# A graph kernel on one core: in both edge loops, TensorE's signals move from the last matmul to a drain behind it

## What is computed

```python
# layer 0, per edge: 8 heads of 16 features
Q, K, V = x @ WQ, x @ WK, x @ WV ;  Eh = edge_attr @ WE
score = exp(clip(sum_head(K[src] * Q[dst] / 4 * Eh), -5, 5))
h = x + segment_sum(V[src] * score, dst) / (segment_sum(score, dst) + 1e-6)
x1 = layernorm(x + batchnorm(h))
# layer 1: graph attention with a softmax over each destination's edges
xl = x1 @ W ;  e = leaky_relu((xl @ att_src)[src] + (xl @ att_dst)[dst])
m = segment_max(e, dst) ;  p = exp(e - m[dst])
out = segment_sum(p / (segment_sum(p, dst)[dst] + 1e-16) * xl[src], dst) + bias
# two dense layers with batch norm and relu follow, and a last layernorm
```

## Time and profile before

| | us |
|---|---|
| median of 3 runs | 5886.87 (5868.76 to 5905.33) |
| profiled execution | 5881.81 |
| its span | 5879.8 |
| busy: TensorE, VectorE, GpSimd, ScalarE | 3739.5, 3231.2, 3271.3, 1157.5 |

### The profile page before, as it was taken

One profiled execution on the slowest core, in us unless ns is written; L12 is line 12 of the kernel. 1 busy time (PEld: TensorE's weight loads), 2 busy tenths in 40 slices (PEclk: granted clock), 3 DMA queues, 4 the chain that ended last, 5 costly groups with the idle time before them and its releaser, 6 DMA issues. The chain is left out here.

```text
span 5879.8 us, 84494 instructions
## 1 busy us (share of the span) xinstructions
PE 3739.5 (64%) x20678; PEld 2886.8 (49%) x20679; DVE 3231.2 (55%) x9533; ACT 1157.5 (20%) x4808; POOL 3271.3 (56%) x3437
## 2 busy tenths in 40 slices
PE   7666656666676666666684656666666566666577
PEld 5444444444454444545453445444444444444455
DVE  4555555555565555555562555555555555555566
ACT  3111111111111111111111222222222222222234
POOL 4555555555555555555535466666666666666641
PEclk8777777777767677766777555555555555555558
DMA  6444444444454444444423222222222222222213
GB/s 234 136 133 138 134 135 136 134 137 140 138 142 134 135 139 132 137 135 139 137 91 115 71 51 50 51 50 50 50 50 50 50 51 50 50 50 51 50 37 136
DMA packets 433128, 592.20 MB, mean 101 GB/s; under 512 B 210923, under 2 KB 291125, under 8 KB 430949
## 3 DMA queue, kind: packets, MB, share of 16 engines
q0 software_dynamic: 132560, 328.87, 21.8%
q1 hardware_dynamic: 298678, 255.32, 15.8%
q10 hardware_dynamic: 1840, 7.43, 0.3%
HBM read 556.41 MB, written 34.03 MB: 100 GB/s over the span
## 5 line engine op out<-in xcount | busy, mean ns | idle before, releaser
L415 POOL DMA_INDIRECT kv_g<-kv_table,idx x1641 | 1559.3, 950 | 1336.6 <-PE ps_sum L507 774.9
L1168 POOL DMA_INDIRECT xg<-xl_table,idx x1661 | 1582.5, 953 | 990.0 <-issue 466.0
L1226 PE MATMUL ps_sum<-pw,xg 128*128 128x64 f32 x3328 | 819.2, 428 | 475.8 <-DVE pws L1367 338.1
L1226 PEld LDWEIGHTS ps_sum<-pw,xg 128*128 128x128 f32 x3328 | 741.0, 328 | 637.7 <-DVE pws L1367 427.0
L507 PE MATMUL ps_sum<-kv_g,hot 128*64 128x136 f32 x3328 | 388.1, 371 | 955.6 <-ACT qw L584 868.4
L507 PEld LDWEIGHTS ps_sum<-kv_g,hot 128*64 128x64 f32 x3328 | 245.1, 176 | 1068.2 <-ACT qw L584 946.1
L489 PE MATMUL ps_pair<-w,eat 128*128 128x128 f32 x3328 | 693.5, 373 | 0.0
L674 DVE TENSOR_TENSOR acc<-acc,ps_turn 128x128 f32 x416 | 119.5, 287 | 1016.7 <-remote 641.8
L489 PEld LDWEIGHTS ps_pair<-w,eat 128*128 128x128 f32 x3328 | 590.1, 267 | 114.2 <-issue 114.2
L1217 PE MATMUL ps_tops<-ident,col 64*128 64x64 f32 x832 | 285.5, 445 | 304.4 <-DVE col L1345 185.2
L1262 ACT COPY third<-newm 128x64 f32 x416 | 102.4, 246 | 1816.5 <-remote 991.2
(11 more groups left out here) (174 smaller groups left out, 5344.9 us busy)
## 6 DMA issues: line engine op xcount, KB each, us to landing
eat<-in_edges SPq DMA_DIRECT2D x416, 256.0 KB
local<-local_table SPq DMA_DIRECT2D x832, 64.0 KB
xg<-xl_table,idx POOLq DMA_INDIRECT x1661
kv_g<-kv_table,idx POOLq DMA_INDIRECT x1641
xw<-in_xt SPq DMA_DIRECT2D x416, 32.0 KB
adw<-ad_row SPq DMA_DIRECT2D x416, 32.0 KB
kv_table<-kv_out SPq DMA_DIRECT2D x25, 512.0 KB
xl_table<-xl SPq DMA_DIRECT2D x25, 264.0 KB, 2.6
```

The lines of the kernel that those rows point to most:

```text
L415: nc.gpsimd.indirect_dma_start(out=kv[:, u, k, 0:2 * D], out_offset=None, in_=m["kv_table"], in_offset=bass.IndirectOffsetOnAxis(ap=idx[:, ...
L1168: nc.gpsimd.indirect_dma_start(out=xg[:, u, k], out_offset=None, in_=m["xl_table"], in_offset=bass.IndirectOffsetOnAxis(ap=idx[:, u // B, ...
L1226: nc.tensor.matmul(ps_sum[:, b, 0:W], xg[:, u, k, 0:D], pw[:, b, k], start=(k == 0), stop=(k == K - 1))
```

## The change

In five places a drain is put on TensorE behind the last matmul of a group, and the signal moves from the matmul to the drain: `q_made`, `summed` and `turned` in `edges0`, `turned` and `summed` in `edges1`. A drain is an instruction of the engine's sequencer that ends when the engine has finished what was issued to it. No matmul, wait, buffer or transfer is changed. The signals outside the two loops' bodies (the stage ahead of the second loop, the two first `spread_out`, the last `spread_max`) stay on matmuls.

```diff
@@ make_q (edges0)
                 for half in range(2):
-                    mm = nc.tensor.matmul(ps_own[at(half, W)], xw[:, u % 4], m["w"][:, WQ], start=True, stop=True)
-                mm.then_inc(q_made, 1)
+                    nc.tensor.matmul(ps_own[at(half, W)], xw[:, u % 4], m["w"][:, WQ], start=True, stop=True)
+                nc.tensor.drain().then_inc(q_made, 1)
@@ sum_up (edges0)
-                        mm = nc.tensor.matmul(ps_sum[at(half, W), b, 0:D + H], hot[:, u % 4, half * 2 + j], kv[:, u, half * 2 + j, D:ROW0],
-                                              start=(j == 0), stop=(j == K // 2 - 1))
-                mm.then_inc(summed, 1)
+                        nc.tensor.matmul(ps_sum[at(half, W), b, 0:D + H], hot[:, u % 4, half * 2 + j], kv[:, u, half * 2 + j, D:ROW0],
+                                         start=(j == 0), stop=(j == K // 2 - 1))
+                nc.tensor.drain().then_inc(summed, 1)
@@ turn_sums (edges0)
-                nc.tensor.matmul(ps_turn[0:H, b, W:2 * W], sums[:, b, D:D + H], halves[:],
-                                 start=True, stop=True).then_inc(turned, 1)
+                nc.tensor.matmul(ps_turn[0:H, b, W:2 * W], sums[:, b, D:D + H], halves[:], start=True, stop=True)
+                nc.tensor.drain().then_inc(turned, 1)
@@ turn_top (edges1)
-                nc.tensor.matmul(ps_top[0:W, u % 2, 0:P], top[:, u % 2], m["ident"][:], start=True, stop=True).then_inc(turned, 1)
+                nc.tensor.matmul(ps_top[0:W, u % 2, 0:P], top[:, u % 2], m["ident"][:], start=True, stop=True)
+                nc.tensor.drain().then_inc(turned, 1)
@@ sum_up (edges1)
-                nc.tensor.matmul(ps_sum[:, b, W:2 * W], ones, pws[:, b], start=True, stop=True).then_inc(summed, 1)
+                nc.tensor.matmul(ps_sum[:, b, W:2 * W], ones, pws[:, b], start=True, stop=True)
+                nc.tensor.drain().then_inc(summed, 1)
```

## The result

| | kernel before | changed kernel |
|---|---|---|
| median (5 runs each), us | 5881.0 (5868.8 to 5905.3) | 5918.9 (5918.2 to 5930.0) |
| ratio | 1 | 1.0065 (95% interval 1.0039 to 1.0091) |
| profiled execution: span, us | 5879.8 | 5916.8 |

Where an execution took over 1.5% more than the fastest of its kernel, the tables leave it out; further down that is one of e1's four (4775.7 us, the one profiled) and one of e6's two (4357.5 us, the one profiled).

What follows compares the result with a forecast made beforehand. A lockstep of gathers and held TensorE signals was taken to bound both loops; 615 + 383 + 40 = 1038 us off 5881.8 gives 4844, so 4850 us for the median, range 4590 to 6100.

Steps and rivals of the forecast that it cites:

- what bounds the kernel: Both loops: lockstep; gathers hold back the signal summed, then GpSimd idles for it, 2.0 and 1.06 us a chunk.
- GpSimd's two rows, 0.95 and 0.30 us: Both loops: a gather's duration and the idle time ahead of it, so four gathers need 5.0 us a chunk.
- I take it that it escapes: Both loops: a drain-given signal uses the sequencer's way and is not held under gathers; 4850 us, chance 0.60.
- 615 + 383 + 40 us: Savings forecast for the first loop, the second loop and the buffered chunks behind the last gather; 1038 us in all.
- B: Rival, both loops: the drain itself is held and TensorE stands still; 1.5 us a chunk, 620 us; chance 0.12.
- later groups run on: Argument against the held-drain rival: the matmul's data must be there, since TensorE's later groups continue.
- A: Rival, both loops: the drain's signal is held like the matmul's; drains add 243 us, 6130 us; chance 0.20.
- C: Rival: signals come at once, but TensorE's first loop falls to 1.2 GHz, 6.9 us a chunk; 5420 to 5500 us; chance 0.08.
- A drain's cost: TensorE, both loops: 0.15 to 0.45 us each, taken as 0.3; 0.9 us a chunk in the first, 0.6 in the second.
- about 6 us: First loop: TensorE's chunk at 1.2 GHz, from 4.94 us for 27 of 36 matmul records.
- The first loop without late signals: First edge loop with drains and prompt signals: 5.5 us a chunk instead of 7.0, saving 615 us.
- The second: Second edge loop with drains and prompt signals: 5.1 us a chunk instead of 6.06, saving 383 us.

Runs made afterwards that it cites:

- e1: Only the first loop's three signal-giving drains added to the kernel before, second loop unchanged; prompt signals: 4658.0 us against 4542.0, ratio 1.025.
- e6: The changed kernel with its five drains, gathers replaced by plain loads of fixed rows (outputs not the reference's); late job: 4264.4 us against 5812.9, ratio 0.734.
- e5: The kernel before, signals on matmuls, gathers replaced by plain loads of fixed rows (outputs not the reference's); late job: 3892.7 us against 5812.9, ratio 0.670.
- e12: Kernel before plus a signal-less drain behind each of the five groups, signals staying on matmuls; late job: 5930.7 us against 5885.1, ratio 1.008.
- e13: Kernel before with one first-loop drain a chunk, signalling for turn_sums and make_q together, summed on its matmul; late job: 5864.6 us against 5885.1, ratio 0.996.
- e8: Kernel before plus the first loop's three drains and two of four line 489 matmuls issued twice; late job: 5943.7 us against 5812.9, ratio 1.024.
- e2: Only the second loop's two signal-giving drains added to the kernel before, first loop unchanged; prompt signals: 4542.0 us against 4542.0, ratio 1.0002.
- e10: Repeat with only the second loop's two signal-giving drains added to the kernel before; prompt job: 4540.4 us against 4541.4, ratio 0.9997.
- e3: Kernel before plus a signal-less drain behind each of the five groups, signals staying on matmuls; prompt job: 4560.3 us against 4542.0, ratio 1.0054.
- e9: Repeat with five signal-less drains added to the kernel before, signals staying on matmuls; prompt job: 4570.7 us against 4541.4, ratio 1.0066.

## Why the prediction was wrong

**Right: what bounds the kernel.** The lockstep of gathers and late signals was read correctly for the trace at hand. e5 takes the gathers away and the lateness is gone; in the prompt jobs the lateness is missing and the kernel takes 4541 us, near the forecast of what the loops would need without it. There GpSimd's two rows, 0.95 and 0.30 us, carry both loops (4.94 us a chunk for the 5.0 of the sum).

**The step that failed** is "I take it that it escapes": that the hold sits on the way from TensorE's array to the semaphore, and a drain passes by it. It rested on one drain behind a loop, where nothing is held, and on ScalarE's and VectorE's signals being prompt. Neither row has a drain of TensorE under gathers. e12 and the timelines show that the completion itself comes late, and a drain waits for just that. So the whole 615 + 383 + 40 us fell away.

**The rivals.** B named the mechanism (the drain is held, TensorE stands still) and mis-sized its price: 1.5 us a chunk, 620 us. What argued against B, "later groups run on", shows that TensorE goes on, and says nothing on the report. The stops are as long as B feared: TensorE sits 744 us idle ahead of line 1218 in the second loop. But it would have idled anyway: in 3300 to 5600 us it is busy for 1385 us now and was for 1396 before, since whoever feeds it waits for the same held report. A's price was the same error on a smaller scale, 243 us for 38 measured. C was right on the clock and on TensorE's chunk in the first loop (6.9 us forecast, 6.94 measured), and wrong in that the second loop gains.

**Why the first loop's mean stays** is open in part. Shown is TensorE's own pace: at 1.2 GHz with three drains a chunk takes 6.7 us without any late signal (e1 from 300 to 450 us; e6, where it is 6.7 to 6.9), and the changed kernel, mostly at 1.2 GHz, ticks at 6.83 us. Shown is also that a quicker TensorE doesn't bring the mean down: with clocks of 0.70 (e13) and 0.79 (e8) more drains are late and the mean is 6.9 and 7.1 us. Why so few are late in the changed kernel's first loop (101 of 1248, against 375 in e8) is not shown, and that the mean came out as before, 6.94 for 6.93, may be chance.

**The terms.** A drain's cost was taken as 0.3 us, between 0.15 and 0.45. Where nothing is held it ends 20 to 55 ns behind the matmul, not 70, and costs 0.11 us uncovered in the second loop (e6 against e5), or nothing beside gathers (e2, e10). Behind the sums of the first loop the 0.3 us were right: line 489 starts 0.07 us before the sums' end in e2 and 0.24 us after it in e1, by the medians. In the timeline above it is 0.59 us, as that drain is itself 0.37 us late. A chunk of the first loop has 32 matmul records (11,896 in 372 chunks), and not the 36 of the prediction; its "about 6 us" at 1.2 GHz goes with 32, as 4.94 us for 27 gives 5.9. The first loop without late signals was put at 5.5 us with three drains; e1 has 5.50 in its profiled, longest execution and some 5.2 in the others. The second was put at 5.1 and measured 4.94. So the sum comes near what the loops do in a prompt job, where the kernel before is fast too; the change itself never ran in one.

The Trainium skill, "PSUM — Partial Sum Buffer", section "Engine vs sequencer instructions", had said to put the increment on the matmul and to use a drain only for a barrier of its own. The runs agree: 1.0065 and 1.010 late, and in a prompt job 1.025 for the first loop alone (e1). What the Trainium skill's "Perfetto Trace Analysis", section "Tensor Engine Instruction (MATMUL, LD_WEIGHTS)", says, that the update follows an acknowledgement of the written bytes, fits signal and drain being late together, though no run shows the acknowledgement itself.

## What to carry to other kernels

If a signal comes late, first find out whether the message is late or the completion: put a drain that signals nothing behind the instruction and see whether the engine's next instruction starts late as well. A drain waits for the same completion, so it can't bring the signal earlier; it adds a stop, and three that give signals took TensorE's granted clock from 0.73 to 0.56 (late) and from 0.85 to 0.68 (prompt, e2 and e1). Look also at how many of the semaphores' records a trace has: here most were missing exactly where reports were late. And run the kernel before in every job: here the conditions of a job are worth 22%, the change 0.65%.

## What the runs showed of the hardware

- In the late jobs a matmul's completion is reported microseconds late while GpSimd issues indirect DMAs (4.4, 4.5 and 7.1 us in the cases above). Behind the sums most reports come 1 to 2 us after a gather's end with no gather running (146 of the 216 late drains of line 1229, 67 of the 68 of line 509); behind `make_q` in e13, 127 of 216 come while one runs. With plain loads of as many rows none is late (e5, e6). VectorE's and ScalarE's signals are prompt in the same traces: from an instruction's end to the recorded update it is 0.01 us at the median.
- Whether this happens at all changes from job to job with the kernel unchanged: 5813 to 5885 us or 4541 us, the same chip number among both. With the lateness goes a loss of over half of the semaphores' records in the trace (36,109 before, 101,982 in e10). The gathers themselves are as long in either: 943/949 ns (shortest and median) in the changed kernel's first loop, 940/946 ns in e1's.
- TensorE's granted clock can answer to short stops. With three drains a chunk it alternates in e1's first loop between slices of the page at 1.2 GHz and slices at 0.8 to 0.9 of 2.4 GHz; with three silent ones it falls little in a prompt job (0.86 in e3, 0.81 in e9) and as far as with the others in a late one (0.57 in e12). In e6 a chunk at the low level (6.7 to 6.9 us) takes 1.6 times one at the high level (4.2 us).
- GpSimd's gathers hide two drains a chunk fully where signals are prompt (e2, e10). The gathers are the larger price: without them, and with rows that need no lookup, the kernel takes 3892.7 us (e5), where with them it takes 5812.9 in the same job and 4541 in a prompt one.
